# Low halves of the softmax weights: half a step by VectorE in four steps of nine, in place of whole steps in two

## The reference

```python
qkv = jnp.einsum('bhwc,oc->bhwo', x, qkv_w) + qkv_b
...
attn = jnp.einsum('bqd,bkd->bqk', q, k)
...
attn = (attn.reshape(B * nh, H, W, H, W) + rel_h[:, :, :, :, None] + rel_w[:, :, :, None, :]).reshape(B * nh, N, N)
attn = jax.nn.softmax(attn, axis=-1)
out = jnp.einsum('bqk,bkd->bqd', attn, v)
...
x = x + _L1_conv_ref(_gn(x), ...)
```

## Time and profile before

| | |
|---|---|
| median of 3 runs | 3379.78 us (3377.91 to 3383.99) |
| the profiled execution | 3383.73 us, of which the trace spans 3381.4 us |
| TensorE busy | 2934.7 us (87%) |
| VectorE busy | 2583.6 us (76%) |
| GpSimd busy | 1923.9 us (57%) |
| ScalarE busy | 1802.1 us (53%) |
| granted TensorE clock, mean | 0.933 |

### The profile page before, as it was taken

How to read it: one execution, slowest core, us unless ns; L and a number is a source line. 1 busy time by engine, 2 the same in 40 slices (tenths; PEclk the granted TensorE clock), 3 DMA queues, 4 the chain that set the end, 5 groups by cost and what they waited for, 6 DMA issues and landing times. The chain is left out here.

```text
span 3381.4 us, 95017 instructions
## 1 busy us (share of the span) xinstructions
PE 2934.7 (87%) x33912; PEld 1907.3 (56%) x33912; DVE 2583.6 (76%) x5459; ACT 1802.1 (53%) x3290; POOL 1923.9 (57%) x1560
## 2 busy tenths in 40 slices
PE   1987999987298848999999999999999999999977
PEld 1554777764154623666566666666656666666644
DVE  6745888866763648988898888898989888889824
ACT  3333667664333512565555656555556565555664
POOL 3453555550303003777777777777777777777772
PEclk9997999998599557999999999999999999999989
DMA  2425655547032984222222222222222222222114
GB/s 114 187 85 134 144 131 142 143 106 259 31 135 68 240 174 130 49 49 49 50 49 50 49 50 49 50 49 50 49 50 49 50 49 50 49 50 49 40 44 140
DMA packets 165484, 295.05 MB, mean 87 GB/s; under 512 B 81546, under 2 KB 115428, under 8 KB 159588
## 3 DMA queue, kind: packets, MB, share of 16 engines
q1 hardware_dynamic: 165076, 289.54, 33.7%
HBM read 189.37 MB, written 85.45 MB: 81 GB/s over the span
## 5 line engine op out<-in xcount | busy, mean ns | idle before, releaser
L1700 POOL TENSOR_TENSOR fprob_low<-fprob 128x768 f16<-128x768 f32 x1008 | 1470.8, 1476 | 570.6 <-ACT fprob L1670 558.8
L1711 DVE TENSOR_REDUCE fpart_max<-fmax_acc 128x1 f32<-128x384 f32 x2592 | 1347.2, 553 | 169.7 <-PE fmax_acc L1552 156.2
L1670 ACT ACTIVATE fprob<-fscores 128x768 f32<-128x768 f32 x1296 | 1031.9, 806 | 769.1 <-PE fscores L1576 768.7
L1552 PE MATMUL fmax_acc<-fk_m,fq_m 128*128 128x384 f16 x2592 | 867.8, 336 | 132.8 <-DVE fpart_max L1711 82.9
L1574 PE MATMUL fscores<-fq_a,fk_a 128*128 128x384 f16 x2592 | 849.7, 328 | 36.2 <-issue 32.2
L1576 PE MATMUL fscores<-fq_b,fk_b 97*128 97x384 f16 x2592 | 853.1, 329 | 0.0
L1600 PE MATMUL fout_acc<-fv,fprob 128*128 128x65 f16 x7776 | 613.7, 191 | 8.2 <-POOL fprob_low L1700 6.6
L1601 PE MATMUL fout_acc<-fv,fprob_low 128*128 128x33 f16 x7776 | 597.2, 179 | 0.0
L1600 PEld LDWEIGHTS fout_acc<-fv,fprob 128*128 128x128 bf16 x7776 | 542.7, 97 | 73.4 <-POOL fprob_low L1700 23.2
L1601 PEld LDWEIGHTS fout_acc<-fv,fprob_low 128*128 128x128 f16 x7776 | 489.3, 96 | 53.5 <-issue 3.4
L1552 PEld LDWEIGHTS fmax_acc<-fk_m,fq_m 128*128 128x128 f16 x2592 | 252.5, 97 | 377.1 <-DVE fpart_max L1711 281.0
(11 more groups left out here) (128 smaller groups left out, 3823.7 us busy)
## 6 DMA issues: line engine op xcount, KB each, us to landing
q_a<-q_hi SPq DMA_DIRECT2D x48, 432.0 KB, 5.8
fq_a<-q_hi SPq DMA_DIRECT2D x48, 432.0 KB, 7.8
q_a<-q_lo SPq DMA_DIRECT2D x24, 432.0 KB, 7.4
row_bias<-x SPq DMA_DIRECT2D x24, 432.0 KB, 7.6
col_bias<-x SPq DMA_DIRECT2D x72, 144.0 KB, 3.8
fq_a<-q_lo SPq DMA_DIRECT2D x24, 432.0 KB, 8.4
fq_a<-col_bias SPq DMA_DIRECT2D x24, 432.0 KB, 12.0
fq_b<-row_bias SPq DMA_DIRECT2D x24, 432.0 KB, 14.8
```

The source lines that it names most:

```text
L1552: nc.tensor.matmul(max_acc[:, bank, 0:PIECE], q_m[:, b, tile * 128:(tile + 1) * 128], k_m[:, b, piece * PIECE:(piece + 1) * PIECE], start= ...
L1670: nc.scalar.activation(prob[:, k % RING, :].rearrange("p (j n) -> p j n", j=2), scores[:, 2 * (k % 2):2 * (k % 2) + 2, 0:UNIT], ACT.Exp).t ...
L1700: engine.tensor_tensor(prob_low[:, k % RING, :], prob[:, k % RING, :], prob[:, k % RING, :].bitcast(BF16)[:, 1::2], ALU.subtract).then_inc ...
L1711: nc.vector.reduce_max(part_max[:, j // PIECES, j % PIECES:j % PIECES + 1], max_acc[:, bank, 0:PIECE], axis=AX.X).then_inc(bank_read, 1)
```

## The change

VectorE no longer takes the low parts of steps 3 and 7 whole. It takes the first of the two key tiles (columns 0 to 383 of 768) in steps 1, 3, 5 and 7, and GpSimd takes the second tile of these steps and both tiles of the other five. The products of `weighted` now wait for GpSimd in every step, and for VectorE as well in the four halved ones. The place in VectorE's list is unchanged: one step later, ahead of that step's `take_row` and reduces.

```diff
--- before.py
+++ after.py
@@ -1358,7 +1358,7 @@
     RING = 3
     LAG = 2
     STEPS = NA * PAIRS
-    OF_DVE = (3, 7)
+    HALF_BY_DVE = (1, 3, 5, 7)
     SUM = 2 * D
 
     STEP_PIECES = 2
@@ -1440,10 +1440,7 @@
     def lows(n, p):
 
         u, k = divmod(p, PAIRS)
-        ours = sum(j <= k for j in OF_DVE)
-        by_dve = (n * NA + u) * len(OF_DVE) + ours
-        by_pool = (n * NA + u) * (PAIRS - len(OF_DVE)) + k + 1 - ours
-        return by_dve, by_pool
+        return (n * NA + u) * len(HALF_BY_DVE) + sum(j <= k for j in HALF_BY_DVE)
 
     def is_first(n):
         return isinstance(n, int) and n == 0
@@ -1581,11 +1578,9 @@
 
 
                 a, k = p // PAIRS, p % PAIRS
-                by_dve, by_pool = lows(n, p)
-                if k in OF_DVE:
-                    pe.wait_ge(low_by_dve, by_dve)
-                else:
-                    pe.wait_ge(low_by_pool, by_pool)
+                if k in HALF_BY_DVE:
+                    pe.wait_ge(low_by_dve, lows(n, p))
+                pe.wait_ge(low_by_pool, n * STEPS + p + 1)
                 if k == 0 and due(n * NA + a - 1):
                     pe.wait_ge(sum_ready, n * NA + a - 1)
                 if k == 0:
@@ -1694,11 +1689,13 @@
         def low_part(engine, n, k, done):
 
             ours = engine is nc.vector
-            if ours != (k % PAIRS in OF_DVE):
+            halved = k % PAIRS in HALF_BY_DVE
+            if ours and not halved:
                 return
+            cut = slice(0, UNIT) if ours else slice(UNIT if halved else 0, SLOT)
             engine.wait_ge(prob_ready, n * STEPS + k + 1)
-            engine.tensor_tensor(prob_low[:, k % RING, :], prob[:, k % RING, :],
-                                 prob[:, k % RING, :].bitcast(BF16)[:, 1::2], ALU.subtract).then_inc(done, 1)
+            engine.tensor_tensor(prob_low[:, k % RING, cut], prob[:, k % RING, cut],
+                                 prob[:, k % RING, :].bitcast(BF16)[:, 1::2][:, cut], ALU.subtract).then_inc(done, 1)
 
 
         @block.vector
```

## The result

The changed kernel took **3395.29 us** (median of 6 runs, 3388.09 to 3403.52), the one before 3383.42 us (6 runs, 3377.91 to 3387.87): a ratio of 1.0039, 95% interval [1.002, 1.0058]. It is slower by about 12 us: small, but clear of the noise. The profiled execution spans 3399.8 us, at a mean granted clock of 0.932.

A forecast was written before the change was run, and what follows sets the result against it. No engine is full; a chain that changes engines sets the unit. +0.11 us over 138 units gives +15, the last stage +2; +17 on the median 3379.78 gives 3397, tilted up to 3400, range 3340 to 3430.

The forecast's parts named there:

- rival 2: Halves of VectorE and GpSimd run side by side, not held up: -0.19 us a unit, 3356, or about 3306; chance 0.07.
- A: Stretch from the end of step 3's exponential to the start of step 8's: 5.91 to 5.68 us, -0.23 a unit.
- B: Stretch from the start of step 8's exponential to VectorE's reduces after `fneg_max`: 2.29 us, unchanged because `fneg_max`'s wait covers delay.
- C: Stretch from the reduces after `fneg_max` to step 2's: +0.43 us from 2.30, VectorE's half of step 1 waiting for GpSimd.
- D: Stretch from step 2's reduces to the end of step 3's exponential: 2.86 us before, -0.09 as a TensorE wait is absorbed.
- Sum: The four stretches of a nine-step unit together: +0.11 us a unit, +15 us over 138 units.
- 138 such units: Nine-step units of stages 0 to 22, six per stage, each counted at 13.37 us before the change.
- The last stage: There the engines' exclusion is the bound; a unit goes from 11.50 to 11.6 to 12.0 us, +2 over six units.
- Rival 3: VectorE's half of step 1 goes ahead while GpSimd is still in step 0: -0.15 us a unit, 3361; chance 0.13.
- Rival 1: GpSimd's half goes first in step 3 or 5, delaying the chain 0.7 to 0.8 us: about 3500; chance 0.12.

The follow-up runs named there:

- experiment 1: The changed kernel with VectorE's four halves made by a one-input reduce in place of the two-input subtraction, output differing; 3335.37 us, ratio to before 0.9854.
- experiment 5: The changed kernel, all four halves kept, with `fneg_max` made by ScalarE in place of VectorE; 3394.71 us, ratio to before 1.0028.
- experiment 2: The changed kernel with the next stage's row maxima sent in two groups of three, not five and one (`LATE = 3`); 3388.98 us, ratio to before 1.0022.
- experiment 8: The changed kernel without step 1's half, with `fneg_max` on ScalarE and row maxima sent three and three (`LATE = 3`); 3327.41 us, ratio to before 0.9839.
- experiment 10: The changed kernel with VectorE's half of step 3 made to wait by semaphore until GpSimd's half is done; 3838.54 us, ratio to before 1.134.
- the kernel with two halves: The changed kernel with VectorE halving only steps 3 and 7, GpSimd taking the other steps whole; 3365.7 us, ratio to before 0.9944.

## Why the prediction was right, and where it wasn't

It said 3400, range 3340 to 3430, and slower by over 0.2% at 0.64. The result is 3395, slower by 0.39%. The sign held, and so did the mechanism inside a unit. The size was right in part by luck: the sum of the unit gave less than forecast, and places that it had left out made up for it.

- **The engines exclude each other** (rival 2, side by side). Shown by experiment 1: one input in place of two, and the halves of both engines fall to their own 546 and 828 ns. For that case the rival had the unit at 13.18 (-0.19); it measured 13.03.
- **A, -0.23: measured -0.20.** The half of step 5 was issued 2.57 after the exponential's end, ends at 3.12 (3.11 forecast), and the copy of the row starts at 3.03. It went ahead of GpSimd's waiting half: GpSimd's five start 1.16, 1.43, 1.13 and 1.52 apart and the last takes 0.83, together 6.06, two halves of them held up by VectorE. The half of step 5 itself took 0.55, no more than one undisturbed (0.56): it came to GpSimd's end just in time, and was hardly held up. The four reduces took 2.17 and not 2.04, since TensorE waited 0.12 for GpSimd's late half of step 3. I had said that this adds none; it fell under the wait of the half of step 5, which covered it.
- **B, 0: measured +0.01**, with `fneg_max` at 0.40 as its cover.
- **C, +0.43: measured +0.33.** This term was mis-sized. I let GpSimd's half of step 1 end 2.40 after the reduces' start; it ended 2.29 after (2024.44 against 2022.15). I had misread the 0.14 by which four low parts took 5.89 and not 5.75 and put it ahead of step 1. It stood behind step 1, where GpSimd waited for the exponential of step 2:

```profile
2013.90 1.47 POOL L1700 TENSOR_TENSOR fprob_low<-fprob 128x768 f16<-128x768 f32 x1
```

That is its low part of step 2, whose exponential is over at 2013.83. The low part of step 1 had started at 2012.33 and ended at 2013.80. With 2012.33 in place of my 2012.45 the working gives 2.61 for C, and 2.63 was measured. VectorE's half ended 0.43 after GpSimd's, as forecast. And the cause reached further than I saw: experiment 5 shows that the end of C is tied to the exponential of step 8 through GpSimd. An error of up to 0.2 on VectorE's side in B or C would not have moved the sum.
- **D, -0.09: measured -0.12.** The pair of step 2 takes 1.01.
- **Sum, +0.11 a unit: measured +0.01 to +0.03**, and so +3 and not +15.
- **The step that was missing** is in the "138 such units": 22 of them run over a stage's end, and I had read no such unit. In 13 the scores of step 0 wait for the transfer of the rows of maxima, and the change took away the cover of that wait (+0.45 each, 6 us). Experiment 2 shows it by taking the wait away, experiment 8 in another kernel. The other nine hold a jump and a fall of TensorE's clock, whose length in the two profiled executions differs by 3.5 us.
- **The last stage, +2:** the unit measured +0.01, and the unit that leads into it +0.55.
- **Rival 3, VectorE ahead in step 1 (0.13):** it didn't happen; the half took 0.77 (above 0.8 had been forecast) and ended after GpSimd's. **Rival 1 (0.12):** GpSimd didn't get in first in steps 3 and 5. Its estimate of 0.7 to 0.8 per unit is not measured. Experiment 10 forces that order in step 3 and costs 3.2 per unit over the 138, but there VectorE is released by a signal and so meets GpSimd's follower too; in the rival it would have stood ready.

Inside a stage A and D give back what C takes; it is the half of step 1 that makes the change a loss, and without it the rest is a gain of 17 us.

## What to carry over

Where VectorE and GpSimd both take subtractions with two inputs in SBUF, place VectorE's where GpSimd stands idle or is released by the same signal, and look for each of them at what GpSimd has queued ahead of it: three of the four halves together gained 17 us, and the fourth, which came behind GpSimd's chain, cost some 30. Of a loop, read the unit over the boundary as well as the usual one; what was covered there by a slower unit comes to light when the unit changes. Before a difference of a few us between two executions is put down to an edit, compare their stretches at a lower clock: here these moved the time by 3.5 us in one pair and by 8 in another. And before taking work off an engine, find which chain ends last at the place where it would be freed: `fneg_max` off VectorE was worth 26 to 30 us in two kernels and nothing in the third.

## What the hardware showed beside that

- A tiny VectorE instruction on 128 x 3 values, with one input in SBUF, is held up by GpSimd as well: `fneg_max` needs 171 ns, took 389 in the mean after the change, 823 in experiment 1 and 739 in the kernel with two halves. In the rows shown it ends where GpSimd's running low part does (2022.24 against 2022.21 after the change). The Trainium skill (SBUF — State Buffer, section "Who interferes with whom") lists `tensor_scalar` among the operations that can take the shared ports in a mode with two of them, and the rows agree.
- A VectorE instruction that is held up gets in when GpSimd's running one ends, ahead of GpSimd's next one: VectorE's half of step 5 ended 0.44 after GpSimd's step 4, while GpSimd's half of step 5 took 1.16 in place of 0.83. But a signal between them is too slow for that: in experiment 10 the 0.10 from GpSimd's end to VectorE's release was enough for GpSimd to start its next instruction, and VectorE stood for all of its 1.43.
- TensorE's granted clock fell after waits of some us in the middle of busy work. After 2.38 us (experiment 10) it went from 1.00 to 0.50 for 3.4 us in most units, and stayed at 1.00 in 16 of 114, which prices the fall at 1.4 us. After the 3.2 to 3.9 us at a jump of the loop it fell for 3.4 or 6.8 us, in eight of nine units before the change and in all nine after it: these units take 16.3 us without a fall, 18.1 to 18.3 in the mean with the shorter and 19.2 with the longer one. After the waits of up to 1.0 us in the units of both kernels it stayed at 1.00.
